# The last 32 hidden units of a gated network: three split products, or one product over 96 rows

## The reference

```python
y = y @ out_proj_w.T + u
zm = rmsnorm(y, post_norm_w)
mlp = jax.nn.gelu(zm @ l1_w.T) * (zm @ l2_w.T) @ l3_w.T
return y + mlp
```

## Time and profile before

| | us |
|---|---|
| median of three runs | 2232.19 |
| the profiled execution, its own time | 2231.43 |
| its span, first to last instruction | 2229.7 |
| TensorE matmuls busy | 2014.4 |
| VectorE busy | 1459.4 |
| ScalarE busy | 1197.0 |
| GpSimd busy | 895.9 |
| gated network (`mlp`), 16 steps | about 312 to 819 of the span |

### The profile page before, as it was taken

One profiled execution on the slowest core, in us unless ns is written; L12 is line 12 of the kernel. 1 busy time (PEld: TensorE's weight loads), 2 busy tenths in 40 slices (PEclk: granted clock), 3 DMA queues, 4 the chain that ended last, 5 costly groups with the idle time before them and its releaser, 6 DMA issues. The chain is left out here.

```text
span 2229.7 us, 39687 instructions
## 1 busy us (share of the span) xinstructions
PE 2014.4 (90%) x12896; PEld 1407.7 (63%) x12960; DVE 1459.4 (65%) x2637; ACT 1197.0 (54%) x2377; POOL 895.9 (40%) x1340
## 2 busy tenths in 40 slices
PE   6886968999999966899999999999999999977997
PEld 4665857888888854565566655666666656534554
DVE  6897444444444335777777777777777877734776
ACT  6775233444544432455665656556565565555564
POOL 3443633555555531233334333443334433332232
PEclk9999988999999978999999999999999999998999
DMA  3343011222222115344343442434433344011222
GB/s 114 120 148 135 31 47 57 77 75 75 75 75 75 47 63 125 74 99 102 78 104 72 108 102 78 100 74 103 107 80 94 75 106 100 22 61 51 91 82 69
DMA packets 104639, 188.05 MB, mean 84 GB/s; under 512 B 27816, under 2 KB 77992, under 8 KB 98344
## 3 DMA queue, kind: packets, MB, share of 16 engines
q1 hardware_dynamic: 104488, 186.14, 31.1%
HBM read 110.23 MB, written 58.79 MB: 76 GB/s over the span
## 5 line engine op out<-in xcount | busy, mean ns | idle before, releaser
L1708 DVE TENSOR_REDUCE at_mneg<-at_ps_s 128x1 f32<-128x384 f32 (+3 forms) x704 | 437.2, 635 | 107.1 <-PE at_ps_s L1346 88.3
L1481 ACT ACTIVATE at_pt<-at_ps_w 128x512 f32<-128x512 f32 x640 | 377.4, 597 | 234.9 <-PE at_ps_w L1357 234.7
L1571 POOL TENSOR_SCALAR_AFFINE_SELECT at_pt<-at_pt 128x256 f32<-128x256 f32 (+1 forms) x640 | 231.8, 365 | 576.3 <-ACT at_pt L1481 573.4
L1345 PE MATMUL at_ps_s<-at_ks,at_qs 96*128 96x128 bf16 (+3 forms) x1024 | 258.8, 306 | 36.1 <-DVE at_mneg L1708 22.3
L1357 PE MATMUL at_ps_w<-at_qs,at_ks 97*128 97x512 bf16 (+3 forms) x1024 | 243.8, 300 | 8.8 <-ACT at_pt L1481 4.8
L1345 PEld LDWEIGHTS at_ps_s<-at_ks,at_qs 96*128 96x128 bf16 x1024 | 85.9, 99 | 225.8 <-DVE at_mneg L1708 140.6
L879 POOL TENSOR_TENSOR ml_m_lo<-ml_m,ml_m_hi 128x512 fp32r<-128x512 f32 x96 | 135.4, 1417 | 196.2 <-ACT ml_m_hi L794 196.0
L1373 PE MATMUL at_ps_o<-at_pt,at_val 128*32 128x512 f32 (+3 forms) x2048 | 166.8, 444 | 9.9 <-POOL at_pt L1571 9.8
L1346 PE MATMUL at_ps_s<-at_mask,at_ident 128*128 128x128 bf16 (+1 forms) x640 | 148.0, 231 | 0.0
L819 ACT ACTIVATE ml_gl<-ml_ps_g 128x512 f32<-128x512 f32 x96 | 56.6, 590 | 167.5 <-PE ml_ps_u L127 163.7
L1357 PEld LDWEIGHTS at_ps_w<-at_qs,at_ks 97*128 97x128 bf16 x1024 | 88.4, 98 | 61.5 <-ACT at_pt L1481 15.1
(11 more groups left out here) (250 smaller groups left out, 5566.7 us busy)
## 6 DMA issues: line engine op xcount, KB each, us to landing
parts_d<-at_parts SPq DMA_DIRECT2D x64, 384.0 KB, 2.5
at_ks<-parts_d SPq DMA_DIRECT2D x192, 128.0 KB, 7.9
at_qs<-parts_d SPq DMA_DIRECT2D x32, 384.0 KB, 5.8
pj_xin<-in_x SPq DMA_DIRECT2D x16, 512.0 KB, 5.1
gate_d<-pj_zc SPq DMA_DIRECT2D x16, 512.0 KB, 2.6
xv_all<-pj_turned_xv SPq DMA_DIRECT2D x16, 512.0 KB, 4.1
ml_turned_y<-xv_all SPq DMA_DIRECT2D x16, 512.0 KB, 3.5
ml_x<-gate_d SPq DMA_DIRECT2D x16, 512.0 KB, 4.3
```

Source lines behind the costliest of these rows:

```text
L1345: pe.matmul(out[:, i, :], qs[par][0:ROWS, h, toks], ks[par][0:ROWS, h, 0:(qt + 1) * P], start=i == 0, stop=False)
L1481: act.activation(pt[u % RING][:], ps_w[u % 2][:], ACT.Exp, scale=SCALE).then_inc(exped, 1)
L1571: pool.affine_select(out=diag, in_=diag, compare_op=ALU.is_ge, fill=0.0, base=0, pattern=pattern, channel_multiplier=-1).then_inc(cut, 1)
L1708: dve.tensor_reduce(mneg[:, g, h0 % HG:h0 % HG + count, qt], view_score(ps_s[s % 2], qt, count), AX_X, ALU.max, negate=True).then_inc(maxe ...
```

## The change

- The products of the last 32 units are kept in one tile `rest` of 96 rows instead of a tile of `m_hi` and one of `m_lo`: rows 0 to 31 the high part, rows 32 to 63 the low part, rows 64 to 95 the high part again.
- The down weights are laid out to fit: the last 32 rows stand three times, the third time as the low part. The zeros of the padding, the two memsets and the semaphore `cleared` go.
- In the down product each block of 128 tokens ends with one matmul over 96 rows in place of three over 128.
- VectorE writes the product k = 5 twice (rows 0 to 31, semaphore `rest_mult`, and rows 32 to 63, `prod_done`).
- ScalarE copies it twice (`rest_parts`: first to rows 64 to 95 of `rest`, semaphore `rest_high`, then, after `prod_done`, rows 0 to 63 of both at once).
- GpSimd subtracts rows 32 to 63 in place, and waits for `rest_high`, for its own low 4 and for its own result.
- The low part of the down weights is made by two instructions instead of one.

```diff
+                elif k == 4:
+                    low_rows = slice(2 * FR, 3 * FR)
+                    whole = slice(0, FT - 1)
+                    dve.tensor_tensor(lo[:, whole, :], raws[k][:, whole, :], hi[:, whole, :].bitcast(F32), ALU.subtract).then_inc(gw.w_low, 1)
+                    dve.tensor_tensor(hi[low_rows, FT - 1, :], raws[k][low_rows, FT - 1, :],
+                                      hi[low_rows, FT - 1, :].bitcast(F32), ALU.subtract).then_inc(gw.w_low, 1)
...
+            def rest_parts(b):
+
+                act.wait_ge(rest_mult, b + 1)
+                wait(act, down_ready, b)
+                act.activation(rest[HI2, :], m[(FT - 1) % 2][HI, :], ACT.Copy).then_inc(rest_high, 1)
+                act.wait_ge(prod_done, FT * (b + 1))
+                act.activation(rest[0:2 * FR, :], m[(FT - 1) % 2][0:2 * FR, :], ACT.Copy).then_inc(m_high, 1)
...
-                product_high(b, par, FT - 1)
+                rest_parts(b)
...
+                    else:
+                        pool.wait_ge(rest_high, b + 1)
+                        pool.wait_ge(m_low, FT * b + k)
+                        pool.tensor_tensor(rest[LO, :], m[k % 2][LO, :], rest[LO, :].bitcast(F32), ALU.subtract).then_inc(m_low, 1)
+                        pool.wait_ge(m_low, FT * (b + 1))
...
-                    mm = products3(pe, ps_o[:, q, :],
-                                   [(m_hi[slot(k, par)][:, toks], m_lo[slot(k, par)][:, toks]) for k in range(FT)],
-                                   [(wd[0][:, k, :], wd[1][:, k, :]) for k in range(FT)])
+                    products3(pe, ps_o[:, q, :],
+                              [(m_hi[slot(k, par)][:, toks], m_lo[slot(k, par)][:, toks]) for k in range(FT - 1)],
+                              [(wd[0][:, k, :], wd[1][:, k, :]) for k in range(FT - 1)], last=False)
+                    mm = pe.matmul(ps_o[:, q, :], rest[0:3 * FR, toks], wd[0][0:3 * FR, FT - 1, :], start=False, stop=True)
...
-            for tail in (m_hi[slot(FT - 1, 0)], m_lo[slot(FT - 1, 0)]):
-                dve.memset(tail[:].bitcast(F32), 0.0).then_inc(cleared, 1)
...
+                        up = ps_g[k % 2][FR:2 * FR, :]
+                        dve.tensor_tensor(m[k % 2][HI, :], gl[k % 2][HI, :], up, ALU.mult).then_inc(rest_mult, 1)
+                        dve.tensor_tensor(m[k % 2][LO, :], gl[k % 2][HI, :], up, ALU.mult).then_inc(prod_done, 1)
...
-        "w_down": tiles(np.concatenate([down, np.zeros((P - FR, D), down.dtype)])),
+        "w_down": tiles(np.concatenate([down] + [down[FW:]] * 2 + [np.zeros((P - 3 * FR, D), down.dtype)])),
```

More of the change, by code:

```diff
@@ L686, in mlp @@
         m = [n.sb(f"m{i}", [P, T]) for i in range(2)]
-        m_hi = [n.sb(f"m_hi{i}", [P, T], F32R) for i in range(FT + 2)]
-        m_lo = [n.sb(f"m_lo{i}", [P, T], F32R) for i in range(FT + 2)]
+        m_hi = [n.sb(f"m_hi{i}", [P, T], F32R) for i in range(FT + 1)]
+        m_lo = [n.sb(f"m_lo{i}", [P, T], F32R) for i in range(FT + 1)]
+        rest = n.sb("rest", [P, T], F32R)
         r = n.sb("r", [P, QT, D])
@@ L706, in mlp @@
             n.sem(s) for s in ("r_set", "stats", "aggr", "lnv_set", "lnr_set", "x1_set"))
-        cleared = n.sem("cleared")
+        rest_mult, rest_high = n.sem("rest_mult"), n.sem("rest_high")
         pool_settled, dve_settled = n.sem("pool_settled"), n.sem("dve_settled")
         block = ctx.enter_context(nc.Block())
+        HI, LO, HI2 = (slice(i * FR, (i + 1) * FR) for i in range(3))
         def slot(k, par):
@@ L793, in product_high @@
                     wait(act, down_ready, b - 1)
-                act.activation(m_hi[slot(k, par)][rows(k), :], m[k % 2][rows(k), :], ACT.Copy).then_inc(m_high, 1)
+                act.activation(m_hi[slot(k, par)][:], m[k % 2][:], ACT.Copy).then_inc(m_high, 1)
+            def rest_parts(b):
[4 more added lines that the diff above has]
+                act.activation(rest[0:2 * FR, :], m[(FT - 1) % 2][0:2 * FR, :], ACT.Copy).then_inc(m_high, 1)
             def norm(b):
@@ L878, in step @@
                     pool.wait_ge(m_high, FT * b + k + 1)
-                    pool.tensor_tensor(m_lo[slot(k, par)][rows(k), :], m[k % 2][rows(k), :],
-                                       m_hi[slot(k, par)][rows(k), :].bitcast(F32), ALU.subtract).then_inc(m_low, 1)
+                    if k < FT - 1:
+                        pool.tensor_tensor(m_lo[slot(k, par)][:], m[k % 2][:], m_hi[slot(k, par)][:].bitcast(F32),
+                                           ALU.subtract).then_inc(m_low, 1)
+                    else:
[3 more added lines that the diff above has]
+                        pool.wait_ge(m_low, FT * (b + 1))
                     if k == 0 and not is_last(b):
@@ L894, in _ @@
             pe.wait_ge(gw.par_loaded, 32)
-            pe.wait_ge(gw.w_low, 8)
-            pe.wait_ge(cleared, 2)
+            pe.wait_ge(gw.w_low, 9)
             def out_product(b):
@@ L1001, in step @@
                     wait(dve, m_low, FT * b + k - 1)
-                    up = ps_u[k % 2][:] if k < FT - 1 else ps_g[k % 2][FR:2 * FR, :]
-                    dve.tensor_tensor(m[k % 2][rows(k), :], gl[k % 2][rows(k), :], up, ALU.mult).then_inc(prod_done, 1)
+                    if k < FT - 1:
+                        dve.tensor_tensor(m[k % 2][:], gl[k % 2][:], ps_u[k % 2][:], ALU.mult).then_inc(prod_done, 1)
+                    else:
+                        up = ps_g[k % 2][FR:2 * FR, :]
+                        dve.tensor_tensor(m[k % 2][HI, :], gl[k % 2][HI, :], up, ALU.mult).then_inc(rest_mult, 1)
+                        dve.tensor_tensor(m[k % 2][LO, :], gl[k % 2][HI, :], up, ALU.mult).then_inc(prod_done, 1)
                     if k >= 2 and is_last(b):
```

## The result

The kernel after takes 2225.16 us (median of nine runs), the kernel before, run beside it, 2239.22. One of the nine runs of the kernel after took 6124.85 us and is left out of the ratio; the median of the other eight is 2224.5. The ratio is 0.9944, 95% interval 0.993 to 0.9958: 0.56% or 12.5 us faster (9.4 to 15.7), where 14.6 us (2217.6 against 2232.19) had been forecast; the two medians differ by 14.1. The time itself lies 1.2 us above the stated range of 2213 to 2224: the difference was forecast well, the level it was taken from was not.

A forecast was written before the change was run, and what follows sets the result against it. The gated network's step was taken as bound by a four-engine chain, then TensorE alone. Terms -15.07 + 0.7 + 0.1 + 0.1 = -14.2 us against 2231.43 gave 2217.2, written as 2217.6; 8-in-10 range 2213 to 2224 us.

The forecast's parts named there:

- What bounds the stage: Gated network step, 28.93 to 29.00 us: 17.5 us handed over between engines up to the down product, then 11.4 us TensorE alone.
- the chain over four engines: Gated network, end of gate/up k = 2 to down product's start: work passed between engines, 17.5 us, TensorE having 0.5 to spare.
- Eight matmuls, 0.942 a step, 15.07 in all: Down product goes from 72 matmuls to 64 at 0.1177 us each; 16 down products save 15.07 us.
- A 96-row matmul at the plain rate: Last matmul of each token block in the down product: 96 rows cost the same as 128, extra price zero.
- rival 2: Down product: switching between 96 and 128 rows stalls TensorE 0.35 us, 64 times, 22.4 us; some 2240 us; chance 0.04.
- The added products and copies, 0.05 a step, between 0 and 0.12: VectorE and ScalarE at k = 5: later layer norm start costs 0.05 us in each of 13 steps, 0.7 us.
- GpSimd, the memsets, the last down product: Gated network and its ends: GpSimd price 0, memsets gain 0, weights' low part 0.1 us, last down product's drain 0.1 us.
- The sum for the stage: Gated network with its borders: -15.07 + 0.7 + 0.1 + 0.1 = -14.2 us.
- from the difference to the time: Whole kernel: -14.2 us against the profiled execution's 2231.43 gives 2217.2; median 0.8 above that execution, so 2217.6 us written.
- rival 3: Whole kernel: matmuls go, but other stretches move with the clock, shifting the result 4 us either way; chance 0.07 beyond forecast's range.
- Rival 1: Gated network: later layer norm delays down product 0.3 to 0.8 us in 13 steps, 2221 to 2228 us; chance 0.13.
- The chances: Whole kernel: faster (below 2221 us) 0.81, the same 0.15, slower 0.04.

## Why the prediction was right and wrong, step by step

- *What bounds the stage* was right: two pieces in a row, the chain over four engines up to the down product's start and TensorE alone behind it. One copy more on the chain costs 0.52 of its time in the open; taking the layer norm off it brings 0.67 a step, in the kernel before 0.62 to 0.64.
- *Eight matmuls, 0.942 a step, 15.07 in all:* right. Alone they bring 0.93 to 0.95.
- *A 96-row matmul at the plain rate:* right, in two ways (the starts 0.12 apart; the step the same with 128 rows), up to some 0.006 us each. The draining of the array that the Trainium skill (TensorEngine Tiling (Array Packing), Key Properties) ties to a change of tiling mode does not show between 96 and 128 rows: rival 2 needed over 0.235 us a round, and four rounds cost 0.02 to 0.04. Rival 2 is out.
- *The added products and copies, 0.05 a step, between 0 and 0.12:* about right in size, but from two errors against each other, so in part by luck. The added work as a whole costs 0.05 to 0.08 a step, 0.7 to 1.0 us in 13 steps. One error: I took VectorE's distance of two instructions from a product and the addition behind it (0.61), and the two products of 32 rows are 0.71 apart, so the layer norm starts 1.96 after product 5, near the late end of the stated 572.19 to 572.32. The other: the 0.52 of cover in the earlier trace rows is that of the tighter of two kinds of steps; in the other kind (0.60) nearly nothing is added. Why the two products do not overlap is open: the first writes rows 0 to 31, the second rows 32 to 63, while all other pairs of VectorE's instructions in this stage that follow each other without a wait start at row 0 and overlap by some 0.08.
- *GpSimd, the memsets, the last down product:* GpSimd's drain is 0.17 (2.5 us in 15 waits before low 5) and hides; the last down product waits 7.0 instead of 6.6, 0.4 where I took 0.1. Up to the gated network 0.50 us more were spent; the last matmuls of the long convolution were already 0.38 late (309.96 against 309.58), which leaves 0.12 for the two instructions of the weights' low part (1.49 and 0.42 us), where 0.1 was taken. The three profiles of before have this border at 320.7 to 322.0, so the 0.12 is not shown to be theirs.
- *The sum for the stage,* -14.2 with the borders, came out as -13.85 in the first pair. The stage itself moves a little: 498.07, 496.51 and 498.08 us in the three profiles of before, 484.22 and 486.34 of after, 484.09 and 483.81 in the two with filled waits, whose code is the same up to there. The means (three of before, four of after) differ by 12.9, near the 12.5 of the ratio.
- *The step that failed is the last one: from the difference to the time.* I added the difference to one profiled execution and a median of three runs that agreed with it (2231.43 and 2232.19), though the third of these runs was at 2239.22. The nine runs beside the kernel after, these three among them, have a median of 2239.22; later ones of the kernel before gave 2235.87, 2238.35 and 2235.02, with runs from 2230.49 to 2242.83. The profile and two of the three runs stood at the low end, so the starting level was 3 to 7 us too low. The text had the spread of 8.5 us in rival 3 but gave it 0.07, treating it as a shift that the change might cause, when it was an uncertainty of the starting level: 2239.22 - 14.2 is 2225.0, and 2225.16 was measured. That the two agree to 0.2 us is luck, since 2239.22 is the highest of the four medians and the difference is known to 3 us only. Rival 1 was not what put the time above the range; the chain's part beyond the 0.7 us that were taken is at most 0.4 us. Rival 3's sign, steps shorter by 0.9 while the whole is not, was half there in the first pair of profiles (6.2 us); the nine runs do not bear it out.
- The chances: 0.81 for faster by over half a per cent. The ratio is 0.9944, interval up to 0.9958, so it fell on that side, narrowly.

## What to carry to other kernels

Cut a pipelined step into the piece where one engine works alone and the piece where a chain hands over: work saved in the first counts in full, work added counts if it falls on the second, however idle its engine is in sum. Where a chain has an instruction that nobody waits for soon (here a layer norm ahead of a gelu), changing their order can bring much of what the work saved brings (here 0.67 a step against 0.88), with the same work done. Forecast a ratio from the changed stage, and give the level its own spread: one profile and the median of three runs are a thin sample of it, and the highest of the three belongs to it as well; the stage table of the same kernel profiled twice tells which stages may move by themselves.

## What the runs showed of the hardware that was not expected

- Two multiplications of 32 x 512 on VectorE, one behind the other, with the same inputs, start 0.71 us apart, against 0.61 between one of 128 x 512 and the addition behind it. The second of the pair writes from row 32 on, the first from row 0.
- A matmul of fp32r over 96 rows has nearly the same rate as one over 128 rows, 0.118 us for 256 columns, in a stream that changes between them: four of them add 0.02 to 0.04 us to a down product of 7.6.
- At the same granted clock of 1.00 the matmuls of 256 columns in the down products have two rates, 0.1177 us nearly always and 0.1133 in a few of them. The granted clock does not tell them apart, and what does is open.
- The same attention takes 1193.5 to 1202.0 us from one execution to another. Through its middle nearly all steps are 70.1 to 70.2 us; up to 3 us of the difference lie ahead of the first layer norm and up to 6.5 in the last two intervals, where the granted clock of the last 130 us is a mean of 0.87 to 0.94. Filling TensorE's waits there, with a wait of 1.8 us added, raised it to 0.97 and gained nothing.
